# Reordering the first group's rows earlier among the weight copies, with fewer idle transposes, in a DLRM tower's opening

## The reference

```
X0 = e                                    # (512, 39, 16)
Xi = einsum('hjk,bjd,bkd->bhd', Wr, X0, Xi) + b      # three times, Wr = W0, W1, W2
z  = concat of Xi.sum(axis=2)                        # (512, 3*128)
h  = relu([z, dense_ctx] @ W_top1 + b_top1)
h  = relu(h @ W_top2 + b_top2);  y = h @ W_top3
```

## Time and profile before

| what | value |
|---|---|
| median of 3 runs | 657.25 us (656.97 to 657.32) |
| profiled execution, first to last instruction | 664.5 us |
| PE busy | 633.7 us, 95% of the span |
| DVE busy | 561.9 us, 85% |
| ACT busy | 557.3 us, 84% |
| POOL busy | 443.1 us, 67% |
| mean granted TensorE clock | 0.995 |

### The profile page before, as it was taken

The page is one execution under the profiler, slowest core; times in us unless marked ns, Lnnn a source line. Parts: engine busy times, 40 slices in busy tenths (PEclk is TensorE's granted clock), DMA queues, the critical chain, the costliest instruction groups (busy, mean ns, idle before and its releaser), DMA issues.

```text
span 664.5 us, 11375 instructions
## 1 busy us (share of the span) xinstructions
PE 633.7 (95%) x2616; PEld 477.0 (72%) x2616; DVE 561.9 (85%) x878; ACT 557.3 (84%) x1940; POOL 443.1 (67%) x504
## 2 busy tenths in 40 slices
PE   2689999999999999999999999999999999989998
PEld 2656767777777777777777777777777777767874
DVE  3538788889899898989898989898989989899890
ACT  2348788989898999999998999998989998999773
POOL 7555897777777778687777787777777535152700
PEclk9799999999999999999999999999999999999999
DMA  8245533242424233242423333323242320200000
GB/s 292 22 61 105 162 38 87 51 87 56 84 56 80 59 58 84 40 102 33 90 41 84 57 86 55 87 52 81 57 85 55 67 68 6 69 27 0 1 0 1
DMA packets 91117, 43.58 MB, mean 66 GB/s; under 512 B 80630, under 2 KB 83780, under 8 KB 88943
## 3 DMA queue, kind: packets, MB, share of 16 engines
q1 hardware_dynamic: 84058, 41.77, 28.1%
q0 software_dynamic: 5120, 1.29, 2.2%
q10 hardware_dynamic: 1904, 0.15, 0.2%
HBM read 36.39 MB, written 1.81 MB: 57 GB/s over the span
## 4 chain that ended last, share of the span: by engine, by line
PE 75%; DVE 8%; ACT 7%; issue 6%; DMA 3%; DVEq 1%; POOL 0%; SPq 0%; another core or an unknown queue 0%
PE yb L1128 16%; PE yb L1124 16%; PE yb L1125 16%; PE p L1089 10%; PE pq L1101 6%; ACT yb L765 5%; DVE x L941 3%; DVE acc L935 3%; DMA gram<-in_L_rec_W_dram 2%; PE yb L1026 2%; DMA emb<-in_table_dram,idx 1%; DVE x1l L896 1%; PE yb L1237 1%; PE p L1182 1%; PE p L1214 1%
## 5 line engine op out<-in xcount | busy, mean ns | idle before, releaser
L765 ACT ACTIVATE yb<-yb,x0t 128x128 f32<-128x128 f32 x1728 | 467.2, 391 | 56.0 <-PE yb L1128 49.6
L935 DVE TENSOR_TENSOR acc<-acc,yb 128x512 f32<-128x512 f32 (+1 forms) x512 | 323.4, 674 | 33.8 <-ACT yb L765 30.9
L1124 PE MATMUL yb<-w1h,x1h 128*128 128x512 f32 (+1 forms) x640 | 293.8, 459 | 5.0 <-DVE acc L935 3.8
L1128 PE MATMUL yb<-w1h,x1l 128*128 128x512 f32 (+1 forms) x640 | 247.4, 387 | 0.0
L1125 PE MATMUL yb<-w1l,x1h 128*128 128x512 f32 (+1 forms) x640 | 247.1, 386 | 0.0
L497 POOL DMA_INDIRECT emb<-in_table_dram,idx x160 | 153.0, 956 | 53.1 <-issue 44.4
L1124 PEld LDWEIGHTS yb<-w1h,x1h 128*128 128x128 f32 x640 | 120.1, 188 | 59.4 <-DVE acc L935 25.3
L1125 PEld LDWEIGHTS yb<-w1l,x1h 128*128 128x128 f32 x640 | 120.5, 188 | 39.6 <-issue 18.0
L1128 PEld LDWEIGHTS yb<-w1h,x1l 128*128 128x128 f32 x640 | 120.1, 188 | 24.8 <-DVE x1l L896 0.4
L568 POOL TENSOR_TENSOR late<-late,x0r 117x512 f32<-117x512 f32 (+1 forms) x105 | 132.7, 1298 | 4.6 <-DMA late<-x_scratch 4.3
L544 POOL TENSOR_TENSOR bdiag<-mask,x0t 128x312 f32<-128x312 f32 x64 | 45.7, 714 | 107.0 <-PE pq L1101 106.4
(11 more groups left out here) (124 smaller groups left out, 377.2 us busy)
## 6 DMA issues: line engine op xcount, KB each, us to landing
late<-x_scratch SPq DMA_DIRECT2D x45, 312.0 KB
late<-x_scratch SPq DMA_DIRECT2D x30, 234.0 KB
x0r<-x_scratch SPq DMA_DIRECT2D x15, 234.0 KB
emb<-in_table_dram,idx POOLq DMA_INDIRECT x160
gram<-in_L_rec_W_dram SPq DMA_DIRECT2D x1, 2496.0 KB
late<-x_scratch SPq DMA_DIRECT2D x15, 156.0 KB
spare<-spare SPq DMA_DIRECT2D x28, 78.0 KB
x_scratch<-emb SPq DMA_DIRECT2D x75, 20.0 KB
```

The costliest lines, as they stand in the source:

```text
L765: op = act.activation(part, part, ACT.Copy, scale=x0t[u][:, t, j:j + 1])
L935: dve.tensor_tensor(part, part, parts(y_bank(t, m), n), ALU.add).then_inc(summed, 1)
L1124: pe.matmul(y[:, 0:w], hi, w1h[:, at:at + w], start=True, stop=False)
L1128: pe.matmul(y[:, 0:w], lo, w1h[:, at:at + w], start=False, stop=True).then_inc(bank_ready, 1)
```

## The change

WARM goes from 24 to 8. In ACT's list `dims_outside` and its two `samples` DMAs go from ahead of turn 7 (W1's sixth bank) to ahead of turn 4 (W1's third), and the two `columns` DMAs from behind the last weight copy to ahead of turn 9 (W1's eighth).

```diff
-WARM = 24
-DIMS_TURN = 7
+WARM = 8
+DIMS_TURN = 4
+COLUMNS_TURN = 9
...
                     dims_outside(0, 0, 0)
                     act.wait_ge(embq_ready, 1)
                     samples(act, 0, 0, range(QUARTERS // 2, QUARTERS))
+                if n == COLUMNS_TURN:
+                    act.wait_ge(embt_in, 16 * QUARTERS)
+                    columns(act, x0a, 0, x0a_in, range(TILES // 2, TILES))
                 copy_weights(n)
-            act.wait_ge(embt_in, 16 * QUARTERS)
-            columns(act, x0a, 0, x0a_in, range(TILES // 2, TILES))
             three_times()
```

## The result

The changed kernel takes 658.64 us (median of 10 runs, 657.31 to 660.75), against 657.18 for the kernel before in the same comparison. The ratio is 1.0026 with a 95% interval of 1.0016 to 1.0035: slower by 1.46 us, where 2.0 us less had been forecast.

A forecast was written before the change was run, and what follows sets the result against it. The opening, mostly a TensorE chain running one after the other into the loop, was taken as the bound. Turning the rows 2.25 us earlier, less half of 0.45 for the clock, gave 657.25 - 2.0 = 655.25 us, range 653.2 to 658.6.

The forecast's parts named there:

- Part 1, the reorder: ACT's list: ahead of the third bank the reorder runs 18.5 to 19.0 in idle time; `embt` is there 4.2 us earlier.
- the sum: Whole kernel: the opening's 2.0 us saving carried over to the median of the runs, 657.25 - 2.0 = 655.25 us.
- I take 1.44, what these very copies did: ACT's fourth and fifth W1 copies: spacing taken as 1.44 us, from bounds of 0.55 and 1.44.
- 4.2 us earlier rows: Opening: `embt`, which the column DMAs wait for, ready at 22.5, 4.2 us earlier than before.
- The third bank pays 1.1 us: ACT's copy of W1's third bank, behind the moved reorder, goes from 19.39 to 20.5.
- The gaps are not in the timed runs at all: Rival on ACT's opening copies: both kernels reorder at 18.5, net between -1 and +1 us, 657.2; chance 0.20.
- The gathers land at 22.77: Slower rival: group 0's gathers land late, third copy at 24.75, rows' turn at 34 to 35; 658.3 to 659; chance 0.05.
- Part 2, the columns: ACT's column DMAs issue from 22.5 to 24.65 under copies lasting to 25.1; eighth bank not held, cost 0.
- the seventh would end at 23.3 and the eighth wait 1.35 until 24.65: ACT's W1 copies at 0.55 each, without the cover of earlier copies: the eighth bank waits for the column DMA issue.
- Part 3, the transposes: TensorE: W2's transposes begin at 25.4, eight idle ones end at 30.95 against 33.21; 2.0 us earlier after the clock's cost.
- The clock: TensorE's granted clock: low at 0.50, rising to 1.00 between 30.4 and 31.2; half of 0.45 us lost on the rows' turn.

The follow-up runs named there:

- gate_open: The changed kernel with POOL's gathers of group 1 released two banks earlier; 657.65 us, ratio to the kernel before 1.0006.
- late_gate: The kernel before with POOL's third and later gathers of group 1 waiting for W1's sixth bank; 659.46 us, ratio 1.0032.
- cols_only: The kernel before with only the column DMAs moved ahead of W1's eighth bank; 660.61 us, ratio 1.0053.
- open_warm24: The changed kernel with POOL's gathers of group 1 released two banks earlier and 24 idle transposes instead of 8; 659.08 us, ratio 1.0029.
- warm8_only: The kernel before with 8 idle transposes in place of 24 and nothing else; 658.24 us, ratio 1.0017.
- ordinary profile of before: The kernel before, unchanged, profiled a second time; 657.49 us, span 655.7.
- free_gather: The kernel before with POOL's gathers of group 2 no longer waiting for DVE's pair chunks; 657.65 us, ratio 1.0006.

## Why the prediction was wrong

- **Part 1, the reorder: failed, and with it the sum.** "I take 1.44, what these very copies did" took the gaps in the earlier trace rows as the kernel's own. In an ordinary execution the third bank is copied at 16.26, and the reorder starts at 18.67 where it stood. The 18.5 forecast for the changed kernel was right (18.77); the start before the change was not 22.77. The 4.2 us earlier rows shrink to 0.33. "The third bank pays 1.1 us" falls with it: copied at 16.26 without the change and at 20.74 with it, that bank pays 4.5. The rival "The gaps are not in the timed runs at all" names this, argued from the span, 7.2 us over the runs, and its times came out: third copy about 16.5 (16.26), columns near 27 (27.12 and 26.79), DVE's end between 27.4 and 30 (27.31 and 30.32). It got 0.20; its net of -1 to +1 leaves POOL out. That 658.64 lies within the 658.3 to 659 of "The gathers land at 22.77" is chance, since they had landed by 18.77.
- **The wait that the move adds was followed to the wrong engines.** Part 1 lists what is queued behind the third bank: ACT's copies, DVE, TensorE. POOL's gathers wait for the same banks and are not named. The trace that the prediction was read from has them doing so, in a POOL row that is not among to the earlier trace rows:

```profile
20.26 0.95 POOL L497 DMA_INDIRECT emb<-in_table_dram,idx  x1 [1.18 <-ACT w1h L691]
```

  That wait, 2.61 us in the changed kernel, is the larger part of the loss: opening it gives back half or more of it (gate_open), and closing it in the kernel before costs 2.6, by its profile 1.0 on POOL's path and 1.2 more behind the fall of the clock (late_gate).
- **Part 2, the columns: cost 0 was wrong.** The issue at 22.70 was forecast well. The cover, copies that last to 25.1, was built on the gaps; without it "the seventh would end at 23.3 and the eighth wait 1.35 until 24.65" is what happened (23.3, and 24.88). The late banks then reach W2's turns and DVE's copies: alone, with the clock low behind them, 3.7 us (cols_only), and in the changed kernel, by the chain of gate_open, the part of the loss that the gate does not explain.
- **Part 3, the transposes: right in kind.** Eight instead of 24 gain where W2's turns are late (1.4 us, open_warm24 against gate_open). In the kernel before they lose (warm8_only), because the three-fold rows are begun at 27.01 as before, so that TensorE waits for them, and the clock falls behind that. The predicted moment of the rows' turn, 30.95, was 28.28; its distance to before was 0.25, not 2.25.
- **The clock.** It was to be low until after 30 and was 1.00 from 22 to 32 in the changed kernel's profile, though TensorE did nothing but transposes up to 30.9. Two of its stretches:

```profile
24.00:26.00 2.00, 1.24 (x9) 0.81 (x8) 0.95 (x2) 1.12 (x3) 1.58 (x2) 1.00 0.36 49
28.00:30.00 2.00, 1.32 (x13) 1.12 (x10) 2.00 (x4) 1.10 (x4) 1.70 (x2) 1.00 0.09 8
```

  The Trainium skill says in "TensorE: Matmul & The Clock Gate", Part 4, that the full clock does not engage for transposes; these rows disagree with it again, as the earlier trace rows did.
- **Which end counts.** The forecast assumed that an opening that ends earlier moves the rest forward by as much. By these runs the opening's end at 40 us is one of three things that the loop starts from. Group 2's gathers at 51 and POOL's list from 52 to 81 are as long, so less time on TensorE in the opening gains little by itself, while a late gather on POOL costs: in late_gate TensorE's first bank of the loop came at 39.89, 0.38 earlier than in the ordinary profile of before, and the kernel was slower.

## What to carry to other kernels

Before a row's gap is spent as a gain, compare the span of the profiled execution with the runs: here it was 9 us too long, and the gap belonged to that execution. When a wait is moved in one engine's list, follow every semaphore behind it, those of engines with much idle time too: POOL was 67% busy and still carried the larger part of the loss. When an edit that removes a plain wait gains nothing, look for the wait that opens elsewhere, and remove both.

## What the runs showed of the hardware that was not expected

- The granted clock fell behind a short pause of TensorE deep in a busy stretch as well: it was 0.50 between 56 and 58 us in late_gate behind a pause of 2.12 us, and 1.00 in the same place behind pauses of 1.48 (the changed kernel) and 0.94 (the ordinary profile of before). The product at 57 us took 1.91 us instead of 1.02. The length of the pause alone does not tell it: behind one of 2.21 us ahead of 22.12 in the ordinary profile of before the clock was 0.50 from 24 to 26 us, and behind one of 3.10 us ahead of 22.19 in the changed kernel it stayed at 1.00.
- Ten gathers issued 1.7 us earlier let ACT's reorder begin only 0.42 us earlier, with the DMA engines 0.82 busy meanwhile (free_gather).
- The column DMAs of ACT issue at 22.70 while ACT still has copies to do that were handed on before; in the ordinary profile of before too, where they stood behind all of them. With and without the change they wait for the same four reordering DMAs, so moving them ahead of three copies brought their issue no earlier; it only put these copies behind it, at 24.88.
